# A graph and expert network on one core: spare TensorE products, two passes moved to ScalarE, and an altered order of small steps

## The reference

```python
edge_index = jnp.stack([src, dst])
x = x + _L0_gnn_ref(_layernorm(x), edge_weight, L0_gnn_bias, edge_index)
x = x + _L0_ffn_ref(_layernorm(x)[None], L0_ffn_wg, L0_ffn_w1, L0_ffn_b1, L0_ffn_w2, L0_ffn_b2)[0]
x = x + _L1_gnn_ref(_layernorm(x), edge_index, L1_gnn_W, L1_gnn_b)
x = x + _L1_ffn_ref(_layernorm(x)[None], L1_ffn_w1, L1_ffn_w2)[0]
```

## Time and profile before

| what | before |
|---|---|
| runs | 1074.06, 1076.82, 1076.93 us, median 1076.82 |
| the profiled execution | 1075.01 us, with a span of 1073.3 |
| PE busy | 971.2 us, 90% of the span |
| DVE busy | 740.9 us, 69% |
| ACT busy | 461.9 us, 43% |
| POOL busy | 132.3 us, 12% |
| mean granted clock of TensorE | 0.965 |

### The profile page before, as it was taken

One profiled execution on the slowest core, in us unless ns is written; L12 is line 12 of the kernel. 1 busy time (PEld: TensorE's weight loads), 2 busy tenths in 40 slices (PEclk: granted clock), 3 DMA queues, 4 the chain that ended last, 5 costly groups with the idle time before them and its releaser, 6 DMA issues.

```text
span 1073.3 us, 17293 instructions
## 1 busy us (share of the span) xinstructions
PE 971.2 (90%) x6726; PEld 531.5 (50%) x6726; DVE 740.9 (69%) x1042; ACT 461.9 (43%) x569; POOL 132.3 (12%) x140
## 2 busy tenths in 40 slices
PE   0799869998499999999959999899999999999997
PEld 0688635554366666555534444444444444444443
DVE  7999858886646666666778773899977555555440
ACT  4279635562244445455432122899822222222221
POOL 6200033321220000010043200011100000000000
PEclk9899979999589999999979999999999999999999
DMA  3747605652677776775456765798613654444531
GB/s 123 234 165 265 202 16 208 244 200 78 234 262 266 253 250 236 241 248 210 159 164 166 192 115 193 251 325 310 212 39 62 126 118 111 111 111 111 112 82 35
DMA packets 166031, 188.90 MB, mean 176 GB/s; under 512 B 126505, under 2 KB 126827, under 8 KB 161871
## 3 DMA queue, kind: packets, MB, share of 16 engines
q1 hardware_dynamic: 159567, 165.47, 49.2%
q0 software_dynamic: 6400, 22.55, 6.9%
HBM read 137.98 MB, written 35.33 MB: 161 GB/s over the span
## 4 chain that ended last, share of the span: by engine, by line
PE 71%; DVE 14%; issue 7%; DMA 5%; ACT 2%; DVEq 0%; POOL 0%; SPq 0%; ACTq 0%; POOLq 0%
PE ps L1083 20%; PE ps L1303 13%; PE ps L1274 13%; PE ps L1189 9%; PE ps L1205 6%; DVE fq L2225 3%; PE ps L1146 2%; PE ps L1256 2%; DVE stats L1725 1%; DMA eo_d<-eo 1%; DMA abs_in<-in_L_ffn_w 1%; DVE w1l L2063 1%; DVE x L2279 1%; PE ps L977 1%; PE ps L968 1%
## 5 line engine op out<-in xcount | busy, mean ns | idle before, releaser
L1303 PE MATMUL ps<-w2q,hqt 128*128 128x512 fp8e4 x640 | 140.8, 380 | 1.4 <-DVE out_t L2328 1.4
L1274 PE MATMUL ps<-w1q,xqt 128*128 128x512 fp8e4 x640 | 139.9, 379 | 0.6 <-issue 0.6
L1606 ACT ACTIVATE hf<-ps,fs 128x512 f32<-128x512 f32 x80 | 54.9, 687 | 183.2 <-PE ps L1274 183.2
L2309 DVE TENSOR_REDUCE hm<-hf 128x1 f32<-128x512 f32 x80 | 54.2, 684 | 74.0 <-ACT hf L1606 74.0
L1274 PEld LDWEIGHTS ps<-w1q,xqt 128*128 128x128 f16 x640 | 62.4, 98 | 75.9 <-issue 1.0
L1303 PEld LDWEIGHTS ps<-w2q,hqt 128*128 128x128 f16 x640 | 62.2, 98 | 75.9 <-DVE out_t L2328 1.9
L1083 PE MATMUL ps<-wt_h,xt 128*128 128x512 f16 x320 | 87.3, 386 | 2.9 <-issue 2.9
L1083 PE MATMUL ps<-gwt_h,xt 128*128 128x512 f16 x320 | 85.9, 384 | 0.9 <-issue 0.9
L1189 PE MATMUL ps<-xdh,w1h 128*128 128x314 f16 x256 | 77.7, 304 | 3.5 <-DVE w1l L2063 2.7
L1189 PE MATMUL ps<-xdh,w1l 128*128 128x314 f16 x256 | 77.1, 301 | 0.0
L1189 PE MATMUL ps<-xdl,w1h 128*128 128x314 f16 x256 | 76.9, 301 | 0.0
(11 more groups left out here) (313 smaller groups left out, 1895.0 us busy)
## 6 DMA issues: line engine op xcount, KB each, us to landing
abs_in<-in_L_ffn_w SPq DMA_DIRECT2D x32, 1024.0 KB, 5.9
wstage<-in_L_ffn_w SPq DMA_DIRECT2D x32, 1024.0 KB, 10.9
fnat_b<-in_L_ffn_w SPq DMA_DIRECT2D x28, 512.0 KB, 6.1
fnat_a<-in_L_ffn_w SPq DMA_DIRECT2D x27, 512.0 KB, 4.9
eo_d<-eo SPq DMA_DIRECT2D x16, 512.0 KB, 2.9
...
```

The costliest lines, as they stand in the source:

```text
L1274: last = mm(ps[:, n % 4, :], xqt[:, u, k, :], w1q[:, k // 2, n * 512:(n + 1) * 512, k % 2], start=(k == 0), stop=(k == KD - 1))
L1303: last = mm(ps[:, 4 + h, :], hqt[:, u, k, :], w2q[:, k // 2, h * 512:(h + 1) * 512, k % 2], start=(k == 0), stop=(k == KF - 1))
L1606: cp(hf[:, i % 2, n * 512:(n + 1) * 512], ps[:, n % 4, :], ACT.Gelu, scale=fs[:, i % 2, 3:4]).then_inc(s_ge, 1)
L2309: last = v.tensor_reduce(hm[:, u, n:n + 1], hf[:, u, n * 512:(n + 1) * 512], AX.X, ALU.max, apply_absolute_value=True)
```

## The change

`kept_busy(n)` is new: n products of 512 columns into bank 0, whose result nobody reads. They stand at six places of TensorE's order. The fill of the last tile of x moves from GpSimd to ScalarE. In the build, ScalarE makes the square of the distance in one pass (`distance`; `w_mid` now holds the negative of the middle) and copies the second table (`second_table`); the second slot's `eligible` moves behind batch 1. GpSimd's first bias addition waits for the first copied transposes. After the first product stage TensorE's degree products move ahead of the one-hot ones, and VectorE's gate and slot steps move behind the list `tok_i`; `rt` moves to memory of its own. `s_asked` is now raised by GpSimd's `iota` behind the third gather. VectorE's order changes ahead of expert 0 and ahead of the second product stage.

```diff
@@ sync: the rows of x
-            sp.wait_ge(s_const, 1)
+            sp.wait_ge(s_loops, 2)
@@ gpsimd
             gather(0)
-            g.memset(x[:, NT - 1, :], 0.0).then_inc(s_const, 1)
...
+            pool.wait_ge(s_xtl, 1)
             biased(0)
             biased(1)
             biased(2)
...
                 if n == 2:
-                    pool.sem_inc(s_asked, 1)
+                    g.iota(iota_s[:, :], [[1, SEL]], base=0, channel_multiplier=0, **ok).then_inc(s_asked, 1)
@@ tensor
+            def kept_busy(n):
+
+                for _ in range(n):
+                    mm(ps[:, 0, :], id16[:, :], at_h[:, 0, 0:512], start=True, stop=True)
+
             def transposes(n, u):
...
                 last.then_inc(s_th, 1)
+                if n in (R_GNN0, R_LIN1):
+                    kept_busy(3)
                 pe.wait_ge(s_xl, n + 1)
...
                 transposes(r, 0)
+                kept_busy(4)
                 for i in range(NT):
...
             pe.wait_ge(s_built, 1)
+            kept_busy(6)
             normalised(R_GNN0, lambda i, u: product(R_GNN0 + i, u, wt_h, wt_l))
...
-            pe.wait_ge(s_ohr, 1)
-            for n in range(2 * NT):
-                last = mm(ps[:, 2, 0:3 * NE], oh_lo[:, n // 2, :, n % 2], oh_hi2[:, n, :], start=(n == 0), stop=(n == 2 * NT - 1))
-            last.then_inc(s_tok, 1)
-
-            pe.wait_ge(s_swp, 1)
-            mm(ps[:, 3, 16:18], ones32[:, :], sw[:, 0:2], start=True, stop=True).then_inc(s_swm, 1)
-
+            pe.wait_ge(s_mmread, 2 + R_GNN0 + NT)
             for i in range(NT):
                 for b in range(NT):
                     for a, t in enumerate((at_h, at_l)):
...
             last.then_inc(s_deg, 1)
 
+            pe.wait_ge(s_ohr, 1)
+            for n in range(2 * NT):
+                last = mm(ps[:, 2, 0:3 * NE], oh_lo[:, n // 2, :, n % 2], oh_hi2[:, n, :], start=(n == 0), stop=(n == 2 * NT - 1))
+            last.then_inc(s_tok, 1)
+
+            pe.wait_ge(s_swp, 1)
+            mm(ps[:, 3, 16:18], ones32[:, :], sw[:, 0:2], start=True, stop=True).then_inc(s_swm, 1)
+
             pe.wait_ge(s_toki, 1)
+            kept_busy(18)
...
             for s in range(3):
                 gathered(0, s)
+                kept_busy(3)
             pairs(pe, expert, NE)
...
+            pe.wait_ge(s_g2r, 3 + 6 * NE)
+            pe.wait_ge(s_stat, 2 * NT + 1)
+            kept_busy(8)
             normalised(R_LIN1, lambda i, u: product(R_LIN1 + i, u, gwt_h, gwt_l))
@@ scalar
                 act.wait_ge(s_gat[k], 48 * r + 48)
+                if k == 0:
+                    distance(k)
                 cp(pk[:, k, 2, :], g_w[:, k, :], ACT.Copy, scale=SW).then_inc(s_pka, 1)
                 act.wait_ge(s_slo, 2 * r + k + 1)
+                if k == 1:
+                    distance(k)
                 cp(pk[:, k, 1, :], s_lo[:, :], ACT.Copy).then_inc(s_pka, 1)
+
+            def distance(k):
+
+                cp(k_q[:, :], g_dst[:, k, :], ACT.Square, bias=w_mid[:, k:k + 1]).then_inc(s_pka, 1)
+
+            def second_table(r):
+
+                act.wait_ge(s_piece, 1 + PLACES * r + 2)
+                cp(tab[:, 1, :, :].rearrange("p a (w c) -> p a w c", c=2),
+                   bank16(piece(1).start).rearrange("p (a c w) -> p a w c", a=4, c=2), ACT.Copy).then_inc(s_pd, 1)
...
+            cp(x[:, NT - 1, :], zero[:, 0:1].to_broadcast([P, D]), ACT.Copy).then_inc(s_loops, 1)
...
                     batch(r, b)
+                    if b == 1:
+                        second_table(r)
@@ vector, packed(r, k)
-                kdo(v.tensor_scalar(k_q[:, :], g_dst[:, k, :], w_mid[:, k:k + 1], None, ALU.subtract))
-                kdo(v.tensor_tensor(k_z[:, :], k_q[:, :], k_q[:, :], ALU.mult))
-                ksteps.inc(v.scalar_tensor_tensor(out=k_v[:, :], in0=k_z[:, :], scalar=WIN * WIN / 4, in1=seen[:, k, :],
-                                                  op0=ALU.is_lt, op1=ALU.mult))
+                dve.wait_ge(s_pka, 6 * r + (5 if k else 1))
+                kdo(v.scalar_tensor_tensor(out=k_v[:, :], in0=k_q[:, :], scalar=WIN * WIN / 4, in1=seen[:, k, :],
+                                           op0=ALU.is_lt, op1=ALU.mult))
@@ vector, the build's loop
-                eligible(r)
+                eligible(r, 0)
                 packed(r, 0)
-                table(r, 0)
+                first_table(r)
                 for b in range(NB):
+                    if b == 16:
+                        dve.wait_ge(s_pd, 2 + PLACES * r + 2)
+                        hold(dve)
                     generate(r, b)
                     if b == 1:
+                        eligible(r, 1)
                         packed(r, 1)
                         next_round()
-                        table(r, 1)
@@ vector, before expert 0
-            for q in range(2):
-                split_low(0, q)
-            for s in range(3):
-                gathered(0, s)
+            split_low(0, 0)
+            gathered(0, 0)
+            split_low(0, 1)
+            gathered(0, 1)
+            gathered(0, 2)
@@ vector, before the second product stage
             mixed(1, 0)
+            norm(R_LIN1, 0, 0)
             mixed(1, 1)
-            norm(R_LIN1, 0, 0)
+            low(R_LIN1, 0)
             mixed_statistics(1)
-            low(R_LIN1, 0)
+            copy_low(R_LIN1, 0)
             norm(R_LIN1, 1, 1)
-            copy_low(R_LIN1, 0)
             low(R_LIN1 + 1, 1)
```

81 lines of the change are left out of this document (40 added, 41 removed).

## The result

The changed kernel takes 1060.32 us, the median of four runs (1062.41, 1060.5, 1060.14, 1060.07), beside a median of 1076.36 for the kernel before on the same chip. The ratio is 0.9855, with a 95% interval from 0.9829 to 0.9882: 1.45% faster, 16 us. The forecast was 1059.0 with a range from 1054 to 1067.

The account below looks back on a forecast made before the run. It took the bound to be TensorE stages joined by stretches where another engine prepares the next, TensorE restarting at half clock. Terms sum to 18.1: 1075.0 - 18.1 = 1056.9, plus 1.8 for the median, 1058.7, said as 1059; range 1054 to 1067.

Parts of the forecast that it names:

- First table: Start of the build: VectorE's path to the first table shortens by moving eligibility, fill, distance and square; 2.7 us gained.
- second table: Build: VectorE no longer waits and copies for table 2, and ScalarE makes the square; net 1.2 us gained.
- Clock in the build: Build, 40 to 42: TensorE's idle gap during table 2 shrinks, so less half clock; 0.6 us, bounds 0 and 1.6.
- Rival (c): Build's end set by weight pieces ScalarE sums, not by VectorE's beginning: 4.5 us lost, 1063; chance 0.08.
- First product stage: Start of the first product stage: 3.9 us sooner, 2.7 from the clock, minus 0.3 for spare products.
- xl term: Before the first product stage: two xl splits no longer beside GpSimd's bias additions, so the first product starts 3.9 us sooner.
- clock term: First product stage: products from 146.40 to 151.8 ran at half rate; 2.7 us back if the clock is high.
- Routing: After the first product stage: three gate and three slot instructions leave the path, twice 0.6; 1.2 us gained.
- Gathers: Before expert 0: holding VectorE until three gathers are issued gains 1.0 us; bounds 2.0 and minus 3.0.
- clock of expert 0: Expert 0, 296.14 to 301.9 at half rate: 2.9 us back if the spare products bring the clock up.
- My chain: Before expert 0: token list, second gather, VectorE's w1l before the second copy, third transposes, first product at 293.9 instead of 296.14.
- Second product stage: Second product stage: start 0.3 to 0.8 sooner and 1.9 of clock; 2.2 us, bounds minus 0.5 and 2.8.

Follow-up runs that it names:

- b_build: The kernel before with only the change's new build parts (ScalarE fill, distance and square, second table, later eligibility pair): 1072.97 us, ratio 0.9972.
- the second trace: The changed kernel run again with no edit: 1063.69 us, ratio 0.987 to the kernel before.

## Why the prediction was right, and where it wasn't

**First table, 2.7, and second table, 1.2.** Right at their places; the first split took 0.29 (19.04) and not 1.25. The first o_key came 2.54 sooner (0.2 less), that of the third batch 3.67 (33.32 against 36.99), where 3.9 were added up. The step that failed is the one behind them, that this arrives at the build's end ("everything behind it is started by semaphores and shifts along"). It did in one trace (b_build, 4.0); in the changed kernel's two traces 0.5 and 0.8 arrived. By my own sign ("if the build ends less than 3 sooner") I was wrong here, though the total came out.

**Clock in the build, 0.6.** Right at its place, and more than taken back later. Half clock from 39.1 to 46.0 became 33.8 to 40.7, as long as before, but 5.3 sooner, while the third batch came only 3.7 sooner: less of the batches fell into it, and the lead grew from 3.7 to 4.4 by the seventh batch (to 4.0 in the second trace). Then 3.4 us from 83.5 became 6.8 from 78.2, 3.4 from 127.9 became 6.8 from 122.6, and 3.4 came new from 102.1; the lead fell at the first two of these. I had looked at one stretch and priced its gap. The stretches move with everything else, and their length differs between kernels.

**Rival (c), 0.08, "the build's end is set by the weight pieces that ScalarE sums".** As I priced it (nothing of 4.5 arrives) it is what two traces show, but its reasoning was neither wholly right nor wrong. The argument against it, that these loads shift along, holds in b_build: there the waits are 1.01, 0.58, 1.07 and 1.23, in the kernel before 1.07, 0.56, 1.04 and 1.23, and the end still moved by 4.0. So the pieces by themselves don't explain why b_build kept its lead and the changed kernel did not. But they do hold the pace: with them out of the way the same build ends 6.9 sooner. It deserved a larger chance; the four waits for abs_in stood in the trace of before, and I never asked what they held up.

**First product stage, 3.9 + 2.7 - 0.3 = 6.3.** Measured 6.5 and 6.2. The xl term was right (3.9 by the run without the wait, against the first trace; 3.5 against the second). The clock term came as forecast in the sum, but by the run without spare products only 1.5 of it belongs to them. "So probably it never falls" was wrong: the clock was at 0.57 from 136 to 140, and the six spare products took 2.74, where they take 1.47 at the full clock (the run without the bias wait); 7 of the 13 ran at the full clock. They still ended in time in the first trace; in the second the stage starts 0.37 later behind xn, so there the 0.3 charged was paid. GpSimd's additions now hold up VectorE's small gate steps, 2.37 where one takes 0.2 (142.08); that was covered, as argued. Here the rule of the Trainium skill, "SBUF — State Buffer", section "SBUF: two separate sides", that the pair of ports is locked for a whole instruction, and the row agree: both instructions took 2.37.

**Routing, 1.2.** Measured 0.83. The instructions left the path, and there were seven of them (a product of gates at 276.77 too). Those behind the places in the lists brought 0.6, as counted. The three gate instructions brought 0.2 and not 0.6: without them VectorE waits 0.43 for ScalarE's high half of the last tile's rows (266.57), a wait that they had filled.

**Gathers, 1.0, and clock of expert 0, 2.9.** Together 3.9 and 3.5 were measured. The start gained 1.1 and 0.7 (12.67 and 13.04 behind tok_i instead of 13.76), but not for the reason given: the hold by itself gives nothing (13.07 without it). Without the spare products it is 12.56 and 12.69, so they bring nothing there. Of the 2.9, 1.1 to 1.5 belong to the spare products. The rest is not the change's. b_build has the old order here and no spare products, and its first product comes 13.22 behind tok_i, the clock rises 3.0 us behind it and not 5.8, and the second layer begins 28.46 behind tok_i and not 30.33. Measured from b_build, the row gained 2.0 and 1.7 instead of 3.9 and 3.5, so that its agreement with the forecast is in part luck: a term that was twice too high met a trace of before that was slow here. My chain had w1l in front of the second copy, and that wait was there, shorter: 0.74.

**Second product stage, 2.2.** Measured 2.8. The start gained 0.89 (8.40 to 7.51 from mv to the first product), above the 0.3 to 0.8 I allowed, and the clock the rest. Without the spare products the stage takes 121.91, as long as in the kernel before, though its start has gained the same 0.89: the clock rises 5.7 us behind the first product then, and 3.9 in the kernel before. The eight spare products took 3.55 at half clock, as priced (3.4).

**Not in the sum: from expert 0 to the mixing, -1.5 and -2.3.** Part of it lies behind the last store: from its issue to the first gather back it is 4.11 (524.90 to 529.01) and was 3.06 (535.90 to 538.96). Over the traces this distance between marks goes from 236.4 to 239.5, with the kernel before at the low end, and b_build, whose code is the same there, at 238.1. So most of it looks like scatter between executions and not like a cost of one edit; no experiment here was made on it. The two rows together say it best: from tok_i to mv it is 266.7 in the kernel before and 266.6 in b_build, and 264.3 and 265.4 in the changed kernel, a gain of 2.4 and 1.3 where 3.9 was forecast.

The total was right because the terms for the two product stages held and the 4 lost in the build was within what a range with rival (c) in it had to allow. That the median of four, 1060.3, lies 1.3 above the forecast is partly luck: the median of all ten runs is 1062.5, nearer to the 1063 of rival (c), and the profiled execution is 5.5 above the 1056.9 worked out for it. Two of the signs that I gave for being wrong came true, the build's end and a later stage that gives back, and the first expert product stood 9.0 earlier and not 13, that of the second stage 11.2 and not 16. (The upper bounds named for the range add up to 2.6 and not to 2.9.) In the profiled execution 12.6 came of 18.1: 4.0 less from the build, 2.1 less behind the experts and in the neighbour sum, 0.5 more elsewhere.

**What stays open.** The build ended at 131.37 and 132.51 in the two kernels with the new build and no spare products, and at 133.5 to 136.0 in the five traces that have at least 28 of them and the same build. The products stand behind the build, so they can't delay it by order. The half clock stretch near 80 lasted 3.4 us in the two and 6.8 in the five. With the weight pieces moved or shortened it lasted 3.4 with all the spare products there, so they don't force the longer one. What makes it longer, or whether it is chance, isn't settled, and with it why the changed kernel loses 4 of its 4.5 in the build.
